# Local-attention half of a transformer block on one core: transposes into another bank, copies moved in the written orders, one bias sum on GpSimd

## The chip, the cores and the metric
The kernel runs on one core of a Trainium2 chip. The metric is the time of one execution on the device, in microseconds (us). TensorE (PE in the profile; PEld its weight loads), VectorE (DVE), ScalarE (ACT), GpSimd (POOL) and SyncE (SP, which only issues transfers) each work through a queue of their own, in order, and meet through semaphores.

## The reference
An input x (8 batches x 1024 tokens x 256) goes through two residual halves. Only the second is touched by the change:

```python
for l in range(2):                       # two layers, on the modulated, normalised x
    h = shift_token(x)                   # second half of the channels comes from the token before
    q, k, v = split(h @ wqkv[l])         # 8 heads of 64
    q, k = rotary_xpos(l2norm(q) * qs, l2norm(k) * ks)
    o = local_attention(q, k, v)         # windows of 128 tokens, each sees itself and the one before
    x = x + o @ wo[l]
    h = layernorm(shift_token(x))        # (h - mean) / sqrt(var + 1e-5) * g + b
    a, g = split(h @ w1[l] + b1[l])
    x = x + (a * gelu(g)) @ w2[l] + b2[l]
```

All of it is float32.

## The kernel before, in words
The first half (up to about 1951 us of the span) is another attention and is not changed. The second half treats the 8 batches as 4 pairs; one batch of a pair belongs to stream X, the other to stream Y, each with SBUF tiles and four PSUM banks of its own (X: 0 to 3, Y: 4 to 7; `bk` is the first). A unit `n` is one window of 128 tokens in one layer; layer `l = n % 2`, so each window goes through layer 0, then layer 1, and then the next window follows: 64 units in each stream.

The order of the work is written out by hand: each engine has a string of steps, and `rounds` goes through it once for every round. A step such as `uTX:0` is step `uT` of stream X for the unit of this round, `d0Y:1` is step `d0` of stream Y for the unit of the round before (the number is the lag). Every engine keeps to its own string; a step starts with waits on counting semaphores. The steps of a unit, in the order of the computation:
- `ln`, `le` (layer 0 only): mean and variance of x on VectorE (`ln`, L1282 and L1285), the power -0.5 on POOL (`ln`, L1531 and L1534), and the modulated `u0` on VectorE (`le`, L1289 to L1293).
- `uT` (TensorE, L792): two 128x128 transposes of the layer's input, `u0` or `u`, into bank bk + 2. `uTc` (VectorE, L1307 and L1310) copies them to SBUF, with the token shift.
- `ga`, `gb_`, `gb` (L799): queries and keys of heads 0-3 (a) and 4-7 (b) into banks bk and bk + 1. `v_`, `v` (L808): values into bank bk + 2. `sqa`, `sqb` (ScalarE, L1001) square, `ssa`, `ssb` (VectorE, L1315) sum, `rqa`, `rka`, `rqb`, `rkb` (POOL, L1541 and L1545) take the power; `rot`, `rs`, `ad`, `kn` with a or b (VectorE, L1323, L1329, L1335, L1341) are the rotation.
- `tqa`, `tka`, `tqb`, `tkb` (TensorE, L820) transpose, `qca`, `kca`, `qcb`, `kcb` (ScalarE, L1008 and L1012) copy to SBUF. `sa`, `sb` (TensorE, L830): the scores of four heads each; `sa` waits for `qca` and `kca`, `sb` for `qcb` and `kcb`.
- `m0`, `m1` (VectorE, L1353 and L1358): mask and maximum. `e0` to `e3` (ScalarE, L1019): exponentials of two heads each; `e0`, `e1` wait for `m0`, `e2`, `e3` for `m1`. `d0` to `d3` (VectorE, L1363 and L1366): reciprocal and scaling of two heads. `p0` to `p3` (TensorE, L838) transpose, `pc0` to `pc3` (ScalarE, L1025) copy.
- `o` (L847), `oc` (ScalarE, L1029), `wo_`, `wo` (L856): attention's output and its projection. `u1` (VectorE, L1370) adds the residual.
- `E`, `sh` (L863, L866): the token shift by matmul. `bnu`, `bns`, `ag` (VectorE, L1374, L1377, L1381): statistics; `rs` (POOL, L1549 and L1552): add 1e-5, power -0.5; `hl` (VectorE, L1385): normalise. `h` (TensorE, L871) transposes it, `hT` (ScalarE, L1033) copies.
- `w10` to `w12` (L881), `ge0` to `ge2` (ScalarE, L1041), `ac0` to `ac2` (VectorE, L1396), `w20` to `w22` (L891, into bank bk + 2): the feed-forward part.
- `ub` (VectorE, L1389): u = u1 + b2. `u2` (VectorE, L1402): u = u + the result of `w2`. `fin` (VectorE, L1300 and L1302), in layer 1, makes the output, which SyncE stores.

The semaphore `u2` counts two for every unit, one of `ub` and one of `u2`; `uT` of the next unit waits for both, in layer 0 too, since its bank is the one that `u2` reads. Around the change TensorE's order is `w21X:1 tkbY:1 w22X:1 uTX:0 sbY:1 gaX:0 p0Y:1 gb_X:0 p1Y:1 gbX:0 v_X:0 p2Y:1 vX:0 p3Y:1 tqaX:0 tkaX:0 oY:1`, and for the other stream `w22Y:1 wo_X:0 uTY:0 woX:0`.

Of the kernel before, what the change touches and what calls it, by code (L numbers as in the profile page):

```python
# [21 lines left out]
ALU = mybir.AluOpType  # L22
# [3 lines left out]
P = 128  # L26
B, T, D = 8, 1024, 256
# [39 lines left out]
def build(nc, x, Wa, ba, We, be, Wi, Wo, Wv, Wout, Wout_sw, head_vec, sgn, wqkv, q_scale, k_scale,  # L67
# [7 lines left out]
    with ctx:  # L75
# [7 lines left out]
        ident = res("ident", [P, P])  # L83
# [33 lines left out]
        b2_sb = res("b2_sb", [P, LAYERS, D])  # L117
# [36 lines left out]
        with ExitStack() as scope:  # L154
# [9 lines left out]
                u=tmp(f"u_s{s}", [P, D]),  # L164
# [408 lines left out]
        def _(pe):  # L573
# [207 lines left out]
            def step_pe(name, w, n):  # L781
# [3 lines left out]
                if name == "uT":  # L785
                    src = w["u0"] if l == 0 else w["u"]
                    if l == 0:
                        pe.wait_ge(w["s_ln0"], it * 3 + 3)
                    if n > 0:
                        pe.wait_ge(w["s_u2"], n * 2)  # L790
                    for k in range(DC):
                        mm = pe.transpose(psum[:, bk + 2, k * P:(k + 1) * P], src[:, k * P:(k + 1) * P], ident[:])  # L792
                    mm.then_inc(w["s_uT_ps"], 1)
                elif name in ("ga", "gb_", "gb"):
                    g = 0 if name == "ga" else 1
# [111 lines left out]
        def _(act):  # L907
# [87 lines left out]
            def step_act(name, w, n):  # L995
# [47 lines left out]
                else:  # L1043
# [10 lines left out]
        def _(dve):  # L1054
# [215 lines left out]
            def step_dve(name, w, n):  # L1270
# [32 lines left out]
                elif name == "uTc":  # L1303
# [4 lines left out]
                        .then_inc(w["s_uT"], 1)  # L1308
                    dve.wait_ge(w["s_uT"], n * 2 + 1)
                    dve.tensor_copy(uT[:, 0:2 * (P + 2)].rearrange("p (a n) -> p a n", a=2)[:, :, 0:P],  # L1310
                                    psum[:, bk + 2, 0:D].rearrange("p (a n) -> p a n", a=2)).then_inc(w["s_uT"], 1)
                elif name in ("ssa", "ssb"):
                    sq = w["pT"][:].rearrange("p h k n -> p (h k n)")[:, g * INNER:(g + 1) * INNER].rearrange("p (h d) -> p h d", d=LD)
                    dve.wait_ge(w[f"s_sq{g}"], n + 1)
# [22 lines left out]
                elif name in ("kna", "knb"):  # L1337
                    k = flat[:, g * 2 * INNER + INNER // 2:g * 2 * INNER + INNER].rearrange("p (h d) -> p h d", d=LD)
                    dve.wait_ge(w[f"s_rope{g}"], n * 4 + 3)
                    dve.wait_ge(w[f"s_rn{g}"], n * 4 + 2)  # L1340
                    dve.tensor_tensor(k, k, w["rn"][:, g * LH + LH // 2:(g + 1) * LH].unsqueeze(2).broadcast_to([P, LH // 2, LD]),  # L1341
                                      ALU.mult).then_inc(w[f"s_rope{g}"], 1)
                elif name in ("m0", "m1"):
                    g = int(name[1])
                    if n == 0:
                        dve.wait_ge(s_mask_in, 80)
                    dve.wait_ge(w[f"s_rn{g}"], n * 4 + 4)
                    dve.wait_ge(w[f"s_s_ps{g}"], n + 1)
                    dve.nop(nofuse=True)
                    for h in range(4 * g, 4 * g + 4):  # L1350
                        at, col, _ = score_place(h)
                        q = g * LH + h % 4
                        ins = dve.tensor_tensor_reduce(out=w["big"][:, h, :], in0=psum[:, bk + at, col:col + 2 * P],  # L1353
                                                       in1=maskv[:, 0 if t == 0 else 2 - own], scale=w["rn"][:, q:q + 1],
                                                       scalar=-3.4e38, op0=ALU.add, op1=ALU.max, accum_out=w["mx"][:, h:h + 1])
                    ins.then_inc(w[f"s_sm{g}"], 1)
                    dve.wait_ge(w[f"s_sm{g}"], n * 2 + 1)
                    dve.tensor_scalar(w["mx"][:, 4 * g:4 * g + 4], w["mx"][:, 4 * g:4 * g + 4], -1.0, None, ALU.mult) \  # L1358
                        .then_inc(w[f"s_sm{g}"], 1)
                elif name in ("d0", "d1", "d2", "d3"):  # L1360
                    m = int(name[1])
                    dve.wait_ge(w["s_exp"], n * 4 + m + 1)
                    dve.reciprocal(w["rz"][:, 2 * m:2 * m + 2], w["z"][:, 2 * m:2 * m + 2]).then_inc(w["s_pn"], 1)  # L1363
                    dve.wait_ge(w["s_pn"], n * 8 + 2 * m + 1)
                    for h in (2 * m, 2 * m + 1):
                        ins = dve.tensor_scalar(w["big"][:, h, :], w["big"][:, h, :], w["rz"][:, h:h + 1], None, ALU.mult)  # L1366
                    ins.then_inc(w["s_pn"], 1)
                elif name == "u1":
                    dve.wait_ge(w["s_wo_ps"], n + 1)
                    dve.tensor_tensor(w["u1"][:, l, own, :], psum[:, bk + 3, 0:D], (w["u0"] if l == 0 else w["u"])[:], ALU.add) \  # L1370
                        .then_inc(w["s_u1"], 1)
                elif name == "bnu":
                    dve.wait_ge(w["s_u1"], n + 1)
                    dve.bn_stats(w["st"][:, 0, :], w["u1"][:, l, own, 0:P]).then_inc(w["s_ln_ag"], 1)  # L1374
                elif name == "bns":
                    dve.wait_ge(w["s_sh_ps"], n + 1)
                    dve.bn_stats(w["st"][:, 1, :], psum[:, bk, 0:P]).then_inc(w["s_ln_ag"], 1)  # L1377
                elif name == "ag":
                    dve.wait_ge(w["s_ln_ag"], n * 3 + 2)
                    dve.nop(nofuse=True)  # L1380
                    dve.bn_aggr(w["mv"][:], w["st"][:].rearrange("p a n -> p (a n)")).then_inc(w["s_ln_ag"], 1)  # L1381
                elif name == "hl":
                    dve.wait_ge(w["s_ln_rs"], n * 2 + 2)
                    for k, src in ((0, w["u1"][:, l, own, 0:P]), (1, psum[:, bk, 0:P])):
                        dve.tensor_scalar(w["hl"][:, k * P:(k + 1) * P], src, w["mv"][:, 0:1], w["rs"][:], ALU.subtract, ALU.mult) \  # L1385
                            .then_inc(w["s_hl"], 1)
                elif name == "ub":
                    dve.wait_ge(w["s_u1"], n + 1)
                    dve.tensor_tensor(w["u"][:], w["u1"][:, l, own, :], b2_sb[:, l], ALU.add).then_inc(w["s_u2"], 1)  # L1389
                elif name in ("ac0", "ac1", "ac2"):  # L1390
                    j = int(name[2])
                    gl = w["pT"][:].rearrange("p h k n -> p (h k) n")
                    dve.wait_ge(w["s_gelu"], n * FC + 2 * j + 2)
                    for m, cc in enumerate((2 * j, 2 * j + 1)):
                        rows = FW if cc < FC - 1 else FR
                        dve.scalar_tensor_tensor(out=gl[0:rows, cc, :], in0=psum[0:rows, bk + G_BANK[j], (2 + m) * P:(3 + m) * P],  # L1396
                                                 scalar=b1_sb[0:rows, l, 0, cc:cc + 1], in1=gl[0:rows, cc, :],
                                                 op0=ALU.add, op1=ALU.mult).then_inc(w["s_act"], 1)
                elif name == "u2":
                    dve.wait_ge(w["s_w2_ps"], n + 1)  # L1400
                    dve.wait_ge(w["s_u2"], n * 2 + 1)
                    dve.tensor_tensor(w["u"][:], psum[:, bk + 2, 0:D], w["u"][:], ALU.add).then_inc(w["s_u2"], 1)  # L1402
                else:
                    raise ValueError(name)

            dve.wait_ge(s_wf, 16 * loads[1])
            dve.wait_ge(s_zero, 5)
            rounds(("rsbY:1 rotbY:1 adbY:1 ac0X:1 knbY:1 ac1X:1 ac2X:1 finY:2 m0Y:1 ubX:1 u2X:1 d0Y:1 uTcX:0 d1Y:1 m1Y:1 rsaX:0 "
                    "ssaX:0 d2Y:1 rotaX:0 d3Y:1 adaX:0 knaX:0 rotbX:0 ssbX:0 rsbX:0 adbX:0 m0X:0 u1Y:1 knbX:0 bnuY:1 bnsY:1 agY:1 "
                    "d0X:0 hlY:1 m1X:0 d1X:0 d2X:0 finX:1 d3X:0 lnY:0 ubY:1 ac0Y:1 ac1Y:1 leY:0 ac2Y:1 u2Y:1 uTcY:0 u1X:0 bnuX:0 "  # L1410
                    "lnX:-1 bnsX:0 agX:0 hlX:0 ssaY:0 rsaY:0 rotaY:0 adaY:0 knaY:0 leX:-1 ssbY:0"), step_dve)
# [3 lines left out]
        def _(gp):  # L1415
# [108 lines left out]
            def step_pool(name, w, n):  # L1524
# [90 lines left out]
```

## Time and profile before
| | us |
|---|---|
| median of 3 runs | 5147.08 (5144.16 to 5147.25) |
| the profiled execution | 5151.58, its span 5149.8 |
| PE busy, whole span | 4820.2 (94%) |
| DVE busy | 3885.7 (75%) |
| ACT busy | 2876.1 (56%) |
| POOL busy | 1178.6 (23%) |

Line 1 of the page gives the busy time of each engine; matmuls overlap, so a busy PE is not one at its peak. The second half of the kernel lies from about 1951 us on; a round in it takes about 49.3 us, and layer 0 and layer 1 alternate. A row in a timeline begins with its start in the span and its length; instructions on one engine may overlap at their ends. In brackets stands the idle time of that engine just before the row, and what ended it.

### The profile page before, as it was taken

The numbers are of one execution on the slowest core, as the hardware profiler recorded it, in microseconds if no ns is written. First come the engines' busy times: TensorE is split into PE (matmuls) and PEld (weight loads), VectorE is DVE, ScalarE is ACT, GpSimd is POOL, SyncE is SP. The second block draws the span as 40 slices with busy tenths as digits, with TensorE's granted clock in tenths as the row PEclk, the third lists the DMA queues.
The fourth block names the chain that finished last, engine by engine and source line by source line (L and its number), as shares of the span: only waits on it lengthen the run. The fifth ranks groups of instructions, "written<-read, shape, count | busy, mean of one in ns | idle before, by whom it ended". The sixth has DMA issues, their size and how long they took to land.

```text
span 5149.8 us, 85248 instructions
## 1 busy us (share of the span) xinstructions
PE 4820.2 (94%) x29996; PEld 2903.7 (56%) x29996; DVE 3885.7 (75%) x10911; ACT 2876.1 (56%) x6033; POOL 1178.6 (23%) x1722
## 2 busy tenths in 40 slices
PE   6799999999999997999999999999999999999998
PEld 2233333333333325777777777777777777777776
DVE  6688878788887865777777777777777777777776
ACT  1566666666666663555555555555555555555554
POOL 2202121121202002222222222222222222222222
PEclk7999999999999998999999999999999999999999
DMA  6333233233323311000000000000000000000000
GB/s 148 73 61 63 40 74 58 50 58 64 64 45 66 47 22 41 6 6 5 8 21 13 7 6 6 7 6 29 7 6 6 5 7 27 8 7 6 6 5 5
DMA packets 156588, 153.87 MB, mean 30 GB/s; under 512 B 25244, under 2 KB 148592, under 8 KB 156032
## 3 DMA queue, kind: packets, MB, share of 16 engines
q1 hardware_dynamic: 156160, 148.42, 14.1%
q8 instruction: 237, 3.88, 0.3%
q14 instruction: 191, 1.56, 0.1%
HBM read 103.49 MB, written 44.09 MB: 29 GB/s over the span
## 4 chain that ended last, share of the span: by engine, by line
PE 74%; DVE 12%; issue 4%; ACT 3%; DMA 2%; SPq 2%; POOL 2%; DVEq 0%; POOLq 0%; ACTq 0%
PE psum L881 13%; PE psum L645 8%; PE psum L663 7%; PE psum L799 7%; PE psum L675 6%; PE psum L891 5%; PE psum L847 5%; PE psum L808 4%; PE psum L838 4%; PE psum L830 3%; DVE big_s L1353 3%; DVE mx L1151 3%; PE psum L856 2%; PE psum L628 2%; PE psum L820 1%
## 5 line engine op out<-in xcount | busy, mean ns | idle before, releaser
L1151 DVE TENSOR_REDUCE mx<-psum 128x1 f32<-128x512 f32 x2048 | 1335.3, 687 | 302.0 <-PE psum L645 297.3
L955 ACT ACTIVATE pr<-psum 128x1024 f32<-128x1024 f32 x1024 | 1022.7, 1024 | 638.7 <-PE psum L663 627.5
L645 PE MATMUL psum<-stack 96*128 96x512 bf16 x2048 | 727.4, 389 | 63.3 <-DMA stack<-parts_d 21.5
L881 PE MATMUL psum<-hlT_s,w_sb 128*114 128x128 f32 (+1 forms) x6144 | 741.6, 274 | 30.0 <-ACT hlT_s L1033 30.0
L881 PEld LDWEIGHTS psum<-hlT_s,w_sb 128*114 128x114 f32 (+1 forms) x6144 | 702.9, 178 | 76.8 <-ACT hlT_s L1033 60.7
L1019 ACT ACTIVATE big_s<-big_s,mxl_s 128x256 f32<-128x256 f32 x1024 | 510.9, 502 | 301.5 <-DVE mxl_s L1358 301.5
L663 PE MATMUL psum<-stack 99*128 99x512 bf16 x2048 | 613.6, 381 | 22.7 <-DMA stack<-mrow 22.1
L645 PEld LDWEIGHTS psum<-stack 96*128 96x128 bf16 x2048 | 196.5, 96 | 749.8 <-DVE mx L1151 286.5
L1545 POOL TENSOR_TENSOR rn_s<-ss_s,neghalf 128x4 f32<-128x4 f32 x512 | 550.9, 1076 | 76.0
L675 PE MATMUL psum<-pr,vg 128*32 128x512 f32 x4096 | 546.7, 606 | 0.4 <-ACT pr L955 0.4
L799 PE MATMUL psum<-wqkv_sb,uT_s 128*128 128x512 f32 x1024 | 507.3, 608 | 0.7 <-DVE uT_s L1310 0.7
L1353 DVE CUSTOM_DVE_ANT_0 big_s<-psum,maskv,rn_s 128x256 f32<-128x256 f32 x1024 | 433.8, 482 | 66.6 <-PE psum L830 66.5
L1001 ACT ACTIVATE pT_s<-psum 128x512 f32<-128x512 f32 x256 | 152.4, 595 | 539.3 <-PE psum L799 539.3
L891 PE MATMUL psum<-w_sb,pT_s 114*128 114x256 f32 (+1 forms) x1536 | 408.1, 388 | 0.0
L1041 ACT ACTIVATE pT_s<-psum,b_sb 114x128 f32<-114x128 f32 (+1 forms) x768 | 238.8, 368 | 214.6 <-PE psum L881 213.9
L1541 POOL TENSOR_SCALAR ss_s<-ss_s 128x4 f32<-128x4 f32 x512 | 147.5, 288 | 922.2 <-DVE ss_s L1315 897.7
L1025 ACT ACTIVATE pT_s<-psum 128x512 f32<-128x512 f32 x512 | 294.4, 588 | 98.3 <-PE psum L838 98.3
L830 PE MATMUL psum<-kT_s,qT_s 64*128 64x256 f32 x2048 | 291.3, 403 | 61.4 <-ACT kT_s L1012 61.4
L838 PEld LDWEIGHTS psum<-ident,big_s 128*128 128x128 f32 x2048 | 250.1, 141 | 148.9 <-issue 102.3
L1366 DVE TENSOR_SCALAR big_s<-big_s,rz_s 128x256 f32<-128x256 f32 x1024 | 315.6, 351 | 18.5 <-DVE rz_s L1363 0.4
L1396 DVE SCALAR_TENSOR_TENSOR pT_s<-psum,b_sb,pT_s 114x128 f32<-114x128 f32 (+1 forms) x768 | 230.6, 346 | 113.9 <-ACT pT_s L1041 113.9
L838 PE MATMUL psum<-ident,big_s 128*128 128x128 f32 x2048 | 309.2, 274 | 6.9 <-DVE big_s L1366 6.8
(160 smaller groups left out, 6755.5 us busy)
## 6 DMA issues: line engine op xcount, KB each, us to landing
stack<-parts_d SPq DMA_DIRECT2D x384, 128.0 KB, 5.7
parts_d<-parts SPq DMA_DIRECT2D x64, 384.0 KB, 3.2
hn<-in_x SPq DMA_DIRECT2D x8, 1024.0 KB, 9.2
xr<-in_x SPq DMA_DIRECT2D x8, 1024.0 KB, 5.4
x_d<-xr SPq DMA_DIRECT2D x8, 1024.0 KB, 9.4
tab<-tab_d SPq DMA_DIRECT2D x32, 256.0 KB, 2.5
out_x<-o_s SPq DMA_DIRECT2D x64, 128.0 KB, 1.7
xs<-x_d SPq DMA_DIRECT2D x8, 896.0 KB, 7.5
```

The source lines that it names most:

```text
L645: pe.matmul(psum[:, to, :], stack[0:KS, g % 2, 0, u % 2, h, a * P:(a + 1) * P], stack[0:KS, g % 2, 1, kh, h, :], start=True, stop=True).th ...
L663: mm = pe.matmul(psum[:, h, :], stack[0:KS + PART, (u // 2) % 2, 1, kc // 4, h, (kc % 4) * P:(kc % 4 + 1) * P], stack[0:KS + PART, (u // 2 ...
L675: mm = pe.matmul(psum[h * VW:(h + 1) * VW, ACC, :], vg[:, (u // 2) % 2, kc, h, :], pr[:, e % 2, h, :], start=(kc == 0), stop=(kc == NT - 1))
L799: mm = pe.matmul(psum[:, bk + g, :], w["uT"][:, l, k * (P + 1):k * (P + 1) + P], wqkv_sb[:, l, k, 0:2 * INNER].rearrange("p (a g n) -> p g ...
L838: mm = pe.transpose(psum[:, bk + P_BANK[m], (2 * (h % 2) + kb) * P:(2 * (h % 2) + kb + 1) * P], w["big"][:, h, kb * P:(kb + 1) * P], ident[:])
L881: mm = pe.matmul(psum[0:rows, bk + G_BANK[j], m * P:(m + 1) * P], w1_sb[:, l, k, col:col + rows], w["hlT"][:, k, :], start=(k == 0), stop= ...
L891: mm = pe.matmul(psum[:, bk + 2, 0:D], hid[0:rows, cc, :], w2_sb[0:rows, l, cc, :], start=(cc == 0), stop=(cc == FC - 1))
L955: act.activation(pr[:, e % 2, 2 * pair:2 * pair + 2, :], psum[:, 2 * pair:2 * pair + 2, :], ACT.Exp, scale=DH ** -0.5).then_inc(s_exp, 1)
L1019: ins = act.activation(w["big"][:, h, :], w["big"][:, h, :], ACT.Exp, bias=w["mx"][:, h:h + 1], accum_out=w["z"][:, h:h + 1])
L1151: dve.tensor_reduce(mx[:, u % 2, m, kh:kh + 1], psum[:, src, :], AX.X, ALU.max).then_inc(s_max, 1)
L1353: ins = dve.tensor_tensor_reduce(out=w["big"][:, h, :], in0=psum[:, bk + at, col:col + 2 * P], in1=maskv[:, 0 if t == 0 else 2 - own], sca ...
L1545: gp.tensor_tensor(w["rn"][:, part], w["ss"][:, part], neghalf[:, 0:LH // 2], ALU.pow).then_inc(w[f"s_rn{g}"], 1)
```

## The change
Four edits, all in the second half.
1. `uT` of layer 0 writes bank bk + 3 in place of bk + 2, and `uTc` reads it there. It no longer waits for `u2` of the unit before, only for `ac0` of that unit (which had read bank bk + 3 last) and for `u0`. `v_`, the next to write bank bk + 2, waits for `u2` now. Layer 1 is as it was.
2. ScalarE: `qcbY` and `kcbY` stand ahead of `e0Y`. VectorE: `uTcX` stands ahead of `d0Y`.
3. `ubX` goes from VectorE to POOL, behind `rqbY`, with a further wait for the last `fin`. `ubY` stays on VectorE.
4. The addend 1e-5 of `rs` goes from POOL to VectorE, into `ag`, for both streams; POOL keeps the power.

```diff
                     if l == 0:
                         pe.wait_ge(w["s_ln0"], it * 3 + 3)
-                    if n > 0:
+                    if n > 0 and l == 0:
+                        pe.wait_ge(w["s_act"], (n - 1) * FC + 2)
+                    elif n > 0:
                         pe.wait_ge(w["s_u2"], n * 2)
                     for k in range(DC):
-                        mm = pe.transpose(psum[:, bk + 2, k * P:(k + 1) * P], src[:, k * P:(k + 1) * P], ident[:])
+                        mm = pe.transpose(psum[:, bk + 3 - l, k * P:(k + 1) * P], src[:, k * P:(k + 1) * P], ident[:])
...
                     if k == 0:
                         pe.wait_ge(w["s_uT"], n * 2 + 2)
+                        if n > 0:
+                            pe.wait_ge(w["s_u2"], n * 2)
...
-            rounds(("ge0X:1 ge1X:1 qcaY:1 kcaY:1 ge2X:1 e0Y:1 qcbY:1 kcbY:1 e1Y:1 sqaX:0 e2Y:1 e3Y:1 pc0Y:1 pc1Y:1 sqbX:0 pc2Y:1 "
+            rounds(("ge0X:1 ge1X:1 qcaY:1 kcaY:1 ge2X:1 qcbY:1 kcbY:1 e0Y:1 e1Y:1 sqaX:0 e2Y:1 e3Y:1 pc0Y:1 pc1Y:1 sqbX:0 pc2Y:1 "
...
-                                    psum[:, bk + 2, 0:D].rearrange("p (a n) -> p a n", a=2)).then_inc(w["s_uT"], 1)
+                                    psum[:, bk + 3 - l, 0:D].rearrange("p (a n) -> p a n", a=2)).then_inc(w["s_uT"], 1)
...
                 elif name == "ag":
-                    dve.wait_ge(w["s_ln_ag"], n * 3 + 2)
+                    dve.wait_ge(w["s_ln_ag"], n * 4 + 2)
                     dve.nop(nofuse=True)
                     dve.bn_aggr(w["mv"][:], w["st"][:].rearrange("p a n -> p (a n)")).then_inc(w["s_ln_ag"], 1)
+                    dve.wait_ge(w["s_ln_ag"], n * 4 + 3)
+                    dve.tensor_scalar(w["rs"][:], w["mv"][:, 1:2], LN_EPS, None, ALU.add).then_inc(w["s_ln_ag"], 1)
                 elif name == "hl":
-                    dve.wait_ge(w["s_ln_rs"], n * 2 + 2)
+                    dve.wait_ge(w["s_ln_rs"], n + 1)
...
-            rounds(("rsbY:1 rotbY:1 adbY:1 ac0X:1 knbY:1 ac1X:1 ac2X:1 finY:2 m0Y:1 ubX:1 u2X:1 d0Y:1 uTcX:0 d1Y:1 m1Y:1 rsaX:0 "
+            rounds(("rsbY:1 rotbY:1 adbY:1 ac0X:1 knbY:1 ac1X:1 ac2X:1 finY:2 m0Y:1 u2X:1 uTcX:0 d0Y:1 d1Y:1 m1Y:1 rsaX:0 "
...
                 elif name == "rs":
-                    gp.wait_ge(w["s_ln_ag"], n * 3 + 3)
-                    gp.nop(nofuse=True)
-                    gp.tensor_scalar(w["rs"][:], w["mv"][:, 1:2], LN_EPS, 1.0, ALU.add, ALU.mult).then_inc(w["s_ln_rs"], 1)
-                    gp.wait_ge(w["s_ln_rs"], n * 2 + 1)
+                    gp.wait_ge(w["s_ln_ag"], n * 4 + 4)
                     gp.nop(nofuse=True)
                     gp.tensor_tensor(w["rs"][:], w["rs"][:], neghalf[:, 0:1], ALU.pow).then_inc(w["s_ln_rs"], 1)
+                elif name == "ub":
+                    gp.wait_ge(w["s_u1"], n + 1)
+                    if l == 0 and it > 0:
+                        gp.wait_ge(w["s_oo"], it * 2)
+                    gp.nop(nofuse=True)
+                    gp.tensor_tensor(w["u"][:], w["u1"][:, l, t % 2, :], b2_sb[:, l], ALU.add).then_inc(w["s_u2"], 1)
...
-            rounds(("rqbY:1 rkaX:0 rqaX:0 rkbX:0 rqbX:0 rsY:1 lnY:0 lnX:-1 rsX:0 rkaY:0 rqaY:0 rkbY:0"), step_pool)
+            rounds(("rqbY:1 ubX:1 rkaX:0 rqaX:0 rkbX:0 rqbX:0 rsY:1 lnY:0 lnX:-1 rsX:0 rkaY:0 rqaY:0 rkbY:0"), step_pool)
```

## Rows read from the trace of the kernel before

**Rows 1.** Busy time of each engine in one pair of rounds (instructions in brackets).
```profile
3501.00:3599.59 98.59, 93.28 (x640) 70.18 (x639) 73.34 (x247) 53.90 (x148) 26.47 (x45) 1.00 0.04 12
```

**Rows 2.** Waits of TensorE, 2200 to 5100: us in total, times, longest.
```profile
PE psum L830 <- ACT kT_s L1012: 55.4, 89, 0.8
PE psum L871 <- DVE hl_s L1385: 36.2, 88, 0.8
PE psum L792 <- DVE u_s L1402: 33.8, 59, 0.7
```

**Rows 3.** Timeline of TensorE, rounds A and B: start, length, instructions, idle before.
```profile
3536.22 0.38 PE L820 MATMUL psum<-ident,big_s 128*128 128x128 f32 x2
...
3538.08 0.41 PE L792 MATMUL psum<-ident,u_s 128*128 128x128 f32 x2 [0.61 <-DVE u_s L1402]
...
3546.49 0.66 PE L820 MATMUL psum<-ident,big_s 128*128 128x128 f32 x4
...
3586.74 0.44 PE L792 MATMUL psum<-ident,u_s 128*128 128x128 f32 x2 [0.54 <-DVE u_s L1402]
3587.55 1.13 PE L830 MATMUL psum<-kT_s,qT_s 64*128 64x256 f32 x8 [0.37 <-ACT kT_s L1012]
```

**Rows 4.** Timeline of ScalarE, round A.
```profile
3536.33 0.51 ACT L1019 ACTIVATE big_s<-big_s,mxl_s 128x256 f32<-128x256 f32 x1 [1.20 <-DVE mxl_s L1358]
...
3537.60 0.37 ACT L1012 ACTIVATE kT_s<-psum 128x256 f32<-128x256 f32 x1
3537.86 0.50 ACT L1019 ACTIVATE big_s<-big_s,mxl_s 128x256 f32<-128x256 f32 x1
```

**Rows 5.** Timeline of VectorE, rounds A and B.
```profile
3536.13 0.17 DVE L1358 TENSOR_SCALAR mxl_s<-mxl_s 128x4 f32<-128x4 f32 x1
...
3537.50 0.42 DVE L1402 TENSOR_TENSOR u_s<-psum,u_s 128x256 f32<-128x256 f32 x1 [0.88 <-PE psum L891]
3537.84 0.16 DVE L1363 RECIPROCAL rz_s<-z_s 128x2 f32<-128x2 f32 x1
...
3539.09 0.16 DVE L1363 RECIPROCAL rz_s<-z_s 128x2 f32<-128x2 f32 x1
...
3539.81 0.48 DVE L1353 CUSTOM_DVE_ANT_0 big_s<-psum,maskv,rn_s 128x256 f32<-128x256 f32 x1
...
3542.20 0.76 DVE L1329 TENSOR_TENSOR big_s<-psum,tab 128x256 f32<-128x256 f32 x2 [0.48 <-ACT pT_s L1001]
...
3588.51 0.17 DVE L1363 RECIPROCAL rz_s<-z_s 128x2 f32<-128x2 f32 x1 [0.18 <-ACT big_s L1019]
...
3591.33 0.76 DVE L1329 TENSOR_TENSOR big_s<-psum,tab 128x256 f32<-128x256 f32 x2 [0.18 <-ACT pT_s L1001]
```

**Rows 6.** Timelines of POOL and VectorE, normalisation of stream Y.
```profile
3553.85 0.30 POOL L1549 TENSOR_SCALAR rs_s<-mv_s 128x1 f32<-128x1 f32 x1 [2.94 <-DVE mv_s L1381]
3554.30 0.55 POOL L1552 TENSOR_TENSOR rs_s<-rs_s,neghalf 128x1 f32<-128x1 f32 x1
...
3554.89 0.35 DVE L1385 TENSOR_SCALAR hl_s<-u_s,mv_s,rs_s 128x128 f32<-128x128 f32 x1 [0.52 <-POOL rs_s L1552]
```

**Rows 7.** Timelines of POOL and TensorE, normalisation of stream X.
```profile
3523.70 0.19 POOL L1549 TENSOR_SCALAR rs_s<-mv_s 128x1 f32<-128x1 f32 x1
3524.04 0.54 POOL L1552 TENSOR_TENSOR rs_s<-rs_s,neghalf 128x1 f32<-128x1 f32 x1
...
3525.34 0.44 PE L871 MATMUL psum<-ident,hl_s 128*128 128x128 f32 x2 [0.41 <-DVE hl_s L1385]
```

**Rows 8.** Timeline of POOL, round A, behind `rqbY`.
```profile
3543.71 0.39 POOL L1541 TENSOR_SCALAR ss_s<-ss_s 128x4 f32<-128x4 f32 x1 [9.89 <-DVE ss_s L1315]
```

**Rows 9.** Groups of instructions by line, POOL, 0 to 2050.
```profile
L1501 POOL TENSOR_TENSOR wga<-wfold,gA 128x512 f32<-128x512 f32 x8 | 10.2, 1270 | 52.6 <-DVE xr L1203 52.6
```

**Rows 10.** One line of VectorE: its durations in ns, least, median and most.
```profile
L1366 DVE TENSOR_SCALAR big_s<-big_s,rz_s x944: 345/352/357, 2204.5 to 5090.8; 128x256 f32<-128x256 f32 x189
```

## The prediction
> **What bounds the kernel now.** I call a round one pass of the written orders. A sum over two neighbouring rounds is needed, since the layer (and with it what is late) alternates. In [rows 1] one such pair takes 98.59 us; TensorE has matmuls in flight for 93.28 of them, VectorE works 73.34, ScalarE 53.90 and POOL 26.47, at a granted clock of 1.00. So TensorE bounds the second half, and time can only come from the 5.3 us in which it stands, or from what sits behind them. The view of waits says which these are [rows 2]: attention scores waiting for the copies of keys (55.4 us in 2900), the transposes of the normalised state waiting for VectorE's normalisation (36.2), and the transposes of the layer's input waiting for `u2` (33.8). The change aims at all three, but not at every instance of them; so I read one pair in order of time on each engine, and then moved its instructions. Round A (3501 to 3550) is the one in which stream X starts layer 0, round B (to 3599.6) the one in which it starts layer 1.
>
> **uTX into the other bank, layer 0 (round A).** TensorE ends w22X, idles 0.61 us for `u2`, then runs uTX, with sbY next [rows 3]. Afterwards uTX needs only u0, ready since the round before. So uTX moves up by the 0.61. sbY behind it needs kcbY: that copy ends at 3537.97 today [rows 4], and by itself would keep sbY at 3538.0, so that less than the 0.61 came through. The new wait of v_X for `u2` has the whole of TensorE's queue behind it, but `u2` is done at 3537.92 [rows 5] and v_X stands behind sbY, gaX, p0Y, gb_X, p1Y and gbX in the queue, sbY alone coming later than that: nothing. Stream Y's uTY already stands behind wo_X; the waits for `u2` number 59 [rows 2], one for each of X's rounds, so Y has none: nothing there. In round B uTX still waits for `u2` (0.54 idle, rows 3).
>
> **qcbY and kcbY ahead of e0Y.** Today the order is e0Y, qcbY, kcbY, e1Y [rows 4]. A copy holds ScalarE 0.26 (3537.60 to 3537.86), and 3536.33 to 3537.60 holds two exponentials and one copy, so e0Y is 1.01. New in A: tkbY's transposes end at 3536.60 [rows 3], qcbY starts at 3536.65, kcbY at 3536.91, and e0Y at 3537.17, 0.84 later than now, since its maxima were ready at 3536.30 [rows 5]. kcbY ends near 3537.3, so sbY is no longer late. In B the idle of 0.37 before sbY [rows 3] goes, and e0Y is hardly touched, as there the maxima come last.
>
> **uTcX ahead of d0Y, ubX off VectorE.** Removing ubX (0.34 of VectorE's time) gives nothing: u2X waits 0.88 for TensorE in A [rows 5]. What counts is when m1Y starts, because VectorE's rsaX, ssaX, d2Y, rotaX, d3Y, adaX, knaX follow m1Y in one run, and at its end tkaX needs knaX: TensorE's four transposes of tqaX and tkaX at 3546.49 take 0.66, tkbY's two 0.38 [rows 3], and I read a short wait for knaX in that.
> - A: today d0Y starts 3537.84, d1Y 3539.09, m1Y 3539.81 [rows 5]. d1Y holds VectorE 0.72, d0Y as much, and uTcX the other 0.53 of the 1.25 between d0Y and d1Y. New: uTcX 3537.84 (uTX is done by then), d0Y 3538.37, d1Y at 3539.09 again if e1Y allows it. e1Y starts 3537.17 + 1.01 = 3538.18 and ends, with its last read-out, at about 3539.28, so d1Y goes to 3539.33 and m1Y to 3540.05, 0.24 later. rsaX idles 0.48 today for the square of gaX; gaX is now 0.61 or more earlier, so rsaX starts where m1Y lets it: 0.48 - 0.24 = 0.24 earlier, up to 0.34 with the 0.10 by which a running queue starts the next instruction before the last one's end. I take 0.30.
> - B: uTX ends at 3586.74 + 0.44 = 3587.18. uTcX 3587.22, d0Y 3587.75, d1Y 3588.47, against 3588.51 today [rows 5]: VectorE's new wait for uTX costs what the old wait for e1Y cost; e1Y itself, no longer behind the copies (0.52), is done in time. rsaX's idle of 0.18 goes as its square comes 0.4 earlier. Gain 0.22 to 0.32, I take 0.26.
> So TensorE gets back 0.61 and 0.37 at the front, and most of that is lost again at p2Y, p3Y and tkaX: VectorE is late next.
>
> **The addend on VectorE.** For Y, POOL's add and its wait take 3553.85 to 3554.30, 0.45 [rows 6]. VectorE's narrow tensor_scalar is not in the trace at 128x1; the nearest row is 128x4 at 0.17 [rows 5], with 0.04 to start, 0.21. Saved 0.24, and hlY waits for exactly this power. But POOL's add took 0.30 there and 0.19 where VectorE stood still [rows 6, 7], because d0X's scalings run beside it; the power will now lie beside them. If it stretches by the same 0.11 the gain is 0.13; if it waits out one scaling (0.357, [rows 10]), it is -0.12 (0.24 - 0.36). Ends -0.12 and 0.24; I take 0.13, in both rounds, 0.26 together. After it hY and w10Y follow, both idle-marked today. d0X itself is put back 0.21, covered by the 0.52 that VectorE idles for the power [rows 6].
> For X, in the round with the extra statistics (lnX ahead of rsX on POOL), POOL's rsX add starts at 3523.70 straight behind lnX and the power at 3524.04 [rows 7]. VectorE's add is done long before, so the power starts at 3523.70: 0.34 of the 0.41 us that TensorE idles before hX. Ends 0.19 (the instruction alone) and 0.34; I take 0.34. In the other round hX shows no idle: nothing. The other hidden work moved by 0.34 still fits: in A VectorE has m0Y done at 3536.30, against u2X at 3537.16.
>
> **ubX on POOL.** Not in the trace at 128x256. A POOL tensor_tensor of 128x512 took 1.27 [rows 9]; at half its width it takes at most that, at least 0.42 (VectorE's own time for it); I use 0.7. POOL idles from 3533.82 (3543.71 - 9.89) to 3543.71 [rows 8], u2X needs `ub` by 3537.16: 2 us of cover at the worst. Its wait on the output's stores' semaphore was met a round before, and rkaX, behind it, needs ssaX much later. Cost 0. No DMA moves, SP's queue is not touched.
>
> **Sum.** 0.30 + 0.26 + 0.26 + 0.34 = 1.16 us for a pair, 32 pairs: 37 us. The profiled execution took 5151.6, the median of the runs 5147.1, so the sum is made on rounds of an execution 0.1% slower, which changes nothing in it: 5147.1 - 37 = **5110**. Its own ends: 0.34 + 0.32 + 0.48 + 0.34 = 1.48 (5100) and 0.24 + 0.22 - 0.24 + 0.19 = 0.41 (5134).
>
> **Rivals.**
> 1. TensorE keeps what it gets at the front: p2Y, p3Y and tkaX are not held by VectorE. 0.61 + 0.37 + 0.26 + 0.34 = 1.58, 51 us, 5096; more if the matmul queue hides less than I think. For it: no idle row stands in front of those transposes. Against: the stretched group at 3546.49. Chance 0.12.
> 2. The reordering is eaten by Y's softmax. e0Y's 0.84 passes in full to m1Y in A (0.48 - 0.84 = -0.36), and in B the 0.54 that VectorE stands for uTX passes too (0.18 - 0.54 = -0.36): -0.72 + 0.60 = -0.12, 4 us slower, 5151. For it: d1Y waits for e1Y in both rounds. Against: in A d0Y's place behind u2X leaves only e1Y's part to count. Chance 0.09.
> 3. Slower: POOL and VectorE shut each other out of SBUF. The power waits for all of d0X: d0X ends today at 3554.37 (3554.89 - 0.52, [rows 6]), so 3554.37 + 0.21 + 0.04 + 0.55 + 0.04 = 3555.21 for hlY, -0.32 per round. And `ub` holds VectorE for its 1.27: A has 1.22 in front of u2X (0.88 idle and ubX's 0.34), so -0.05; B has ubX's 0.34 for certain, so -0.93. 0.25 + (0.26 - 0.93) - 0.64 + 0.34 = -0.72 per pair, +23 us, 5170. With the power's part in full it decides from about 0.6 us of holding. Against: VectorE's scalings took 345 to 357 ns whether or not POOL worked beside them [rows 10]; for: POOL's own add was stretched. Chance 0.06. The Trainium skill, SBUF — State Buffer, section "Who interferes with whom", says that the shared port pair is an exclusive lock and the later one is blocked for the whole instruction, against a two-input or 2-port VectorE operation; by that rule the power in rows 6 would wait for a scaling to end, and this rival is its extreme. The 0.11 of stretch in the trace speaks for a block that is short, and on POOL's side.
> 4. POOL's power is stretched and the addend loses for Y (its lower end): 0.30 + 0.26 - 0.24 + 0.34 = 0.66, 5126. For it: the stretch in rows 6. Against: 0.36 is three times that stretch. Chance 0.15.
>
> **Numbers.** My forecast 0.58. Range for 8 in 10: 5093 to 5142, which takes in its ends, cases 1 and 4 and part of the way to case 2. Differences under 0.2% (10 us) are about what a measurement of this kernel can't tell from none. Faster by more: 0.58 + 0.15 + 0.12 = 0.85, same 0.09, slower 0.06.
>
> **What would show it.** Per pair 97.4 us; no idle before uTX in one of two rounds; the waits for keys falling from 1.87 to about 1.5 us a pair, with only those before sbX (0.75) left; rsX's power 0.34 earlier; new stalls before p2Y, p3Y or tkaX of 0.2 to 0.4. Wrong if m1Y starts more than 0.5 later behind w22X than now, if `ub` takes over 2 us, or if VectorE's instructions beside it stretch.

## The result, and the profile after

| | us |
|---|---|
| before, 4 runs | 5147.16 (5144.16 to 5147.73) |
| after, 4 runs | 5176.57 (5173.22 to 5179.21) |
| after divided by before | 1.0054, 95% interval 1.0042 to 1.0067 |
| profiled execution after | 5173.22, its span 5171.4 |

The change makes the kernel 29 us slower, where 37 us faster was forecast. The page's first line gives the busy time of each engine, its share of the span and the instructions:

```profile
PE 4847.7 (94%) x29996; PEld 2893.7 (56%) x29996; DVE 3889.9 (75%) x10975; ACT 2882.0 (56%) x6033; POOL 1195.4 (23%) x1658
```

POOL's busy time rose by 17 us, by what was given to it. PE's rose by 27 (4820.2 before), with the same 29996 matmuls; so matmul groups take longer, and the loss need not show as idle time. One pair of rounds, the view of [rows 1]:

```profile
3494.70:3594.20 99.50, 94.41 (x638) 70.01 (x638) 73.59 (x248) 54.10 (x149) 27.01 (x42) 1.00 0.10 30
```

The pair takes 99.50 in place of 98.59, 0.91 more, at the same granted clock of 1.00; times 32 it is 29 us, the measured loss. (The two profiled executions lie only 21.6 apart, 5171.4 and 5149.8, so for these two traces the pair is on the high side.) Within the pair TensorE's busy time rose by 1.13 and its idle time fell from 5.31 to 5.09. TensorE's waits in 2200 to 5100, the view of [rows 2] (total, times, longest):

```profile
PE psum L842 <- DVE big_s L1370: 48.3, 59, 1.1
PE psum L834 <- ACT kT_s L1016: 43.4, 58, 0.8
...
PE psum L794 <- DVE u_s L1408: 15.5, 30, 0.5
PE psum L875 <- DVE hl_s L1391: 12.5, 57, 0.6
```

All three waits at which the change aims fell: keys from 55.4 to 43.4, the normalised state from 36.2 to 12.5, `u2` from 33.8 to 15.5. In their place stands one that had no row before: the transposes `p2Y` wait for VectorE's scaling, 48.3 us, 59 times, once in each round. Waits alone therefore don't give the bill; it is made below from starts, which take in both the idle time and the stretched groups. Why `p2Y` waits is told by the timeline of ScalarE in round A. First the kernel before, between `ge2X` and `e0Y`; the second row here stands just ahead of the one that opens [rows 4]:

```profile
3533.21 0.63 ACT L1041 ACTIVATE pT_s<-psum,b_sb 114x128 f32<-114x128 f32 x2 [0.79 <-PE psum L881]
3533.85 1.28 ACT L1019 ACT_TABLE_LOAD   x1
```

Then the kernel after, same place of the round:

```profile
3543.29 0.38 ACT L1012 ACTIVATE qT_s<-psum 128x256 f32<-128x256 f32 x1 [2.81 <-PE psum L824]
3543.57 0.38 ACT L1016 ACTIVATE kT_s<-psum 128x256 f32<-128x256 f32 x1
3543.97 1.28 ACT L1023 ACT_TABLE_LOAD   x1
3545.26 0.51 ACT L1023 ACTIVATE big_s<-big_s,mxl_s 128x256 f32<-128x256 f32 x1
```

ScalarE must load another table between the Gelus (`ge`) and the exponentials. The load stands right ahead of the first exponential, whatever is in between. Before, that was in ScalarE's idle time behind `ge2X`, 1.2 us of it still left over [rows 4]. Now ScalarE idles 2.81 us for `tkbY` (both copies wait for both pairs of transposes), copies, and only then loads, 1.28 us, with `e0Y` behind it. VectorE in the same round:

```profile
3546.39 0.17 DVE L1367 RECIPROCAL rz_s<-z_s 128x2 f32<-128x2 f32 x1 [1.28 <-ACT big_s L1023]
...
3548.10 0.48 DVE L1357 CUSTOM_DVE_ANT_0 big_s<-psum,maskv,rn_s 128x256 f32<-128x256 f32 x1
```

And TensorE, first before, from w22X to oY in round A and in round B, then after, the same:

```profile
3536.44 1.03 PE L891 MATMUL psum<-w_sb,pT_s 114*128 114x256 f32 x4
...
3547.08 1.97 PE L847 MATMUL psum<-pT_s,v_s 128*64 128x128 f32 x32
...
3585.17 1.03 PE L891 MATMUL psum<-w_sb,pT_s 114*128 114x256 f32 x4
...
3596.21 1.97 PE L847 MATMUL psum<-pT_s,v_s 128*64 128x128 f32 x32
```

```profile
3543.09 1.03 PE L895 MATMUL psum<-w_sb,pT_s 114*128 114x256 f32 x4
3543.96 0.38 PE L794 MATMUL psum<-ident,u_s 128*128 128x128 f32 x2
3544.27 1.14 PE L834 MATMUL psum<-kT_s,qT_s 64*128 64x256 f32 x8
...
3552.05 0.66 PE L842 MATMUL psum<-ident,big_s 128*128 128x128 f32 x4 [1.11 <-DVE big_s L1370]
...
3553.97 0.90 PE L824 MATMUL psum<-ident,big_s 128*128 128x128 f32 x4
3554.79 1.97 PE L851 MATMUL psum<-pT_s,v_s 128*64 128x128 f32 x32
...
3592.67 1.03 PE L895 MATMUL psum<-w_sb,pT_s 114*128 114x256 f32 x4
...
3604.37 1.97 PE L851 MATMUL psum<-pT_s,v_s 128*64 128x128 f32 x32
```

`d0Y` waits 1.28 for `e0Y`, `m1Y` starts 5.01 behind w22X (3548.10 - 3543.09) where it was 3.37 (3539.81 - 3536.44), and `p2Y` makes TensorE stand 1.11. Behind it the group of `tqaX` and `tkaX` takes 0.90, where it took 0.66 [rows 3]. The front is as forecast: `uTX` and `sbY` follow w22X with no idle. In round B `uTX` still waits for `u2`, as forecast, `sbY` no longer waits, and `p2Y` makes TensorE stand 0.53.

The bill for a pair, from w22X's start to oY's: 11.70 in A (3554.79 - 3543.09) and in B (3604.37 - 3592.67), against 10.64 (3547.08 - 3536.44) and 11.04 (3596.21 - 3585.17) before: 1.06 + 0.66 = 1.72 lost. Behind that, `hY` idles 0.20 or 0.21 in place of 0.41 in both rounds, and `hX` none in place of 0.41: 0.83 won. 0.9 is left, the 0.91 of the pair.

### The profile page after: what moved, and what is told of

It reads as the page before. It is cut to its first block, busy times and chain, and to the rows that moved or that the text cites. A ratio compares the mean times of both kernels' runs of the same rounds, so it can differ in the third digit from the quotient of the medians.

```text
span 5171.4 us, 85310 instructions
## 1 busy us (share of the span) xinstructions
PE 4847.7 (94%) x29996; PEld 2893.7 (56%) x29996; DVE 3889.9 (75%) x10975; ACT 2882.0 (56%) x6033; POOL 1195.4 (23%) x1658
## 3 DMA queue, kind: packets, MB, share of 16 engines
q14 instruction: 191, 1.56, 0.1%
## 4 chain that ended last, share of the span: by engine, by line
PE 72%; DVE 13%; ACT 7%; issue 3%; DMA 2%; SPq 2%; POOL 0%; DVEq 0%; POOLq 0%; ACTq 0%
PE psum L885 13%; PE psum L645 8%; PE psum L663 7%; PE psum L675 7%; PE psum L895 6%; PE psum L851 5%; PE psum L801 4%; PE psum L834 4%; DVE big_s L1357 4%; PE psum L812 3%; PE psum L842 3%; DVE mx L1155 3%; ACT big_s L1023 3%; PE psum L824 2%; PE psum L860 2%
## 5 line engine op out<-in xcount | busy, mean ns | idle before, releaser
L663 PE MATMUL psum<-stack 99*128 99x512 bf16 x2048 | 614.0, 381 | 21.6 <-DMA stack<-mrow 21.0
L842 PEld LDWEIGHTS psum<-ident,big_s 128*128 128x128 f32 x2048 | 238.6, 142 | 234.7 <-DVE big_s L1370 194.3
```

The source lines that it names most:

```text
L663: mm = pe.matmul(psum[:, h, :], stack[0:KS + PART, (u // 2) % 2, 1, kc // 4, h, (kc % 4) * P:(kc % 4 + 1) * P], stack[0:KS + PART, (u // 2 ...
L842: mm = pe.transpose(psum[:, bk + P_BANK[m], (2 * (h % 2) + kb) * P:(2 * (h % 2) + kb + 1) * P], w["big"][:, h, kb * P:(kb + 1) * P], ident[:])
```

## The experiments

Ratios are against the kernel before on the same chip, with 95% intervals; its medians there were 5150.69 (e1 to e4), 5150.15 (e5 to e8) and 5151.78 us (e9 to e11). The theory: the table's load, put on the way to `e0Y`, costs all of it. The rival: it is the longer path of `e0Y` itself, or VectorE's new order, or POOL's sum, and the load changes nothing.

**e1_order_back**: the change, with ScalarE's old order.

```diff
-ge2X:1 qcbY:1 kcbY:1 e0Y:1 e1Y:1
+ge2X:1 e0Y:1 qcbY:1 kcbY:1 e1Y:1
```

> The changed kernel with ScalarE's order as it was before (e0Y ahead of qcbY and kcbY); all other edits stay. Theory T (the load of the exponential's table, 1.28 us, stands right ahead of the first exponential, so that the new order puts it behind kcbY and on the path to d0Y, m1Y and p2Y): all of the loss goes, and the other edits show. In round A sbY still waits for kcbY, 0.4 us gained; round B nothing; hY 0.2 in each round; hX 0.4: 1.2 us for a pair, 39 us under before, about 5108. Rival D (VectorE's uTcX ahead of d0Y, or the sum on POOL, makes VectorE late): little changes, about 5170.

Measured 5123.27 (5121.42 to 5126.0), ratio 0.9948 (0.9934 to 0.9961). The sign turns: ScalarE's order holds the loss. But 27 us are won, not what I expected. TensorE's row shows where the rest is:

```profile
3522.04 1.13 PE L834 MATMUL psum<-kT_s,qT_s 64*128 64x256 f32 x8 [0.74 <-ACT kT_s L1016]
```

`uTX` has moved up, but `sbY` behind it waits 0.74 for `kcbY`, which stands behind `e0Y`. From w22X to `sbY` is 1.99 (3522.04 - 3520.05), as before (3538.41 - 3536.44 = 1.97). `e0Y` itself starts 0.30 behind w22X here (at 3520.35), where it started 0.11 ahead of it [rows 4]: TensorE came forward by 0.41 at `hX`, and the maxima that `e0Y` waits for did not. The addend alone gives 31 us (e6 below); beside it the bank brings nothing more without the copies' move.

**e2_early_load**: the change, with one narrow exponential, whose result nothing reads, right behind `ge2X`. It pulls the load there.

```diff
+            warm = tmp("warm", [P, 1])
...
+                elif name == "warm":
+                    act.activation(warm[:], zero[:, 0:1], ACT.Exp)
...
-ge2X:1 qcbY:1 kcbY:1 e0Y:1 e1Y:1
+ge2X:1 warmY:1 qcbY:1 kcbY:1 e0Y:1 e1Y:1
```

> The changed kernel with one narrow exponential (128x1, its result unused) right behind ge2X, ahead of qcbY and kcbY, whose only use is to draw the table's load forward to there. T: the load lies in ScalarE's idle time again, and the prediction's own sum comes out with the measured terms of the addend: 0.30 + 0.26 + 0.42 + 0.41 = 1.4 us for a pair, 45 us under before, about 5102. D: no change, about 5176.

Measured 5100.66 (5097.72 to 5104.27), ratio 0.9903 (0.989 to 0.9917): 50 us faster than before, 1.5% faster than the change. ScalarE, TensorE and VectorE in round A:

```profile
3508.26 0.62 ACT L1048 ACTIVATE pT_s<-psum,b_sb 114x128 f32<-114x128 f32 x2 [0.79 <-PE psum L886]
3508.90 1.28 ACT L1009 ACT_TABLE_LOAD   x1
3510.19 0.20 ACT L1009 ACTIVATE warm<-zero 128x1 f32<-128x1 f32 x1
3511.69 0.38 ACT L1015 ACTIVATE qT_s<-psum 128x256 f32<-128x256 f32 x1 [1.29 <-PE psum L825]
3511.97 0.38 ACT L1019 ACTIVATE kT_s<-psum 128x256 f32<-128x256 f32 x1
3512.23 0.51 ACT L1026 ACTIVATE big_s<-big_s,mxl_s 128x256 f32<-128x256 f32 x1
```

```profile
3511.49 1.03 PE L896 MATMUL psum<-w_sb,pT_s 114*128 114x256 f32 x4
3512.36 0.38 PE L795 MATMUL psum<-ident,u_s 128*128 128x128 f32 x2
3512.67 1.13 PE L835 MATMUL psum<-kT_s,qT_s 64*128 64x256 f32 x8
...
3521.75 1.42 PE L852 MATMUL psum<-pT_s,v_s 128*64 128x128 f32 x22
```

```profile
3515.06 0.48 DVE L1360 CUSTOM_DVE_ANT_0 big_s<-psum,maskv,rn_s 128x256 f32<-128x256 f32 x1
```

The load fits into the idle time with 1.29 to spare. `e0Y` starts 0.74 behind w22X, `m1Y` 3.57, oY 10.26.

**e3_order_alone**: the kernel before, with ScalarE's new order and nothing else.

```diff
-ge2X:1 e0Y:1 qcbY:1 kcbY:1 e1Y:1
+ge2X:1 qcbY:1 kcbY:1 e0Y:1 e1Y:1
```

> The kernel before with ScalarE's new order alone (qcbY and kcbY ahead of e0Y). T: e0Y starts 2.1 us later in A (0.84 for the copies, 1.28 for the load), and uTcX stands behind d0Y here, so gaX is late by 1.6 in A and 1.1 in B: 2.7 us for a pair, 87 us over before, about 5234. D: this order does no harm, 5130 to 5150.

Measured 5267.53 (5265.61 to 5271.26), ratio 1.0228 (1.0214 to 1.0242): 117 us slower. The late `e0Y` costs even more here, as `uTcX` stands behind `d0Y`, and so `gaX` is late with it. It is some 30 us more than expected; the last section says where most of them are.

**e4_bank_alone**: the kernel before, with the bank and its waits alone.

```diff
-                    if n > 0:
+                    if n > 0 and l == 0:
+                        pe.wait_ge(w["s_act"], (n - 1) * FC + 2)
+                    elif n > 0:
                         pe.wait_ge(w["s_u2"], n * 2)
...
-                        mm = pe.transpose(psum[:, bk + 2, k * P:(k + 1) * P], src[:, k * P:(k + 1) * P], ident[:])
+                        mm = pe.transpose(psum[:, bk + 3 - l, k * P:(k + 1) * P], src[:, k * P:(k + 1) * P], ident[:])
```

> The kernel before with layer 0's transposes in bank bk + 3 alone, with its waits. Both theories: uTX and sbY move up in A, but gaX waits for uTcX, which stands behind d0Y on VectorE and ends at 3539.18: gaX 0.24 earlier, 8 us under before, about 5139. If TensorE's gain came through in full (0.61): 5127; if it doesn't count at all: 5147.

Ratio 0.9985 (0.9976 to 0.9994), 7 us faster: clearly there and small. The wait for `u2` in A turns into one for keys; before there were 89 of these, 55.4 us [rows 2], and now

```profile
PE psum L834 <- ACT kT_s L1016: 64.6, 118, 0.7
```

**e5_order_alone_early_load**: e3 with e2's narrow exponential.

```diff
-ge2X:1 e0Y:1 qcbY:1 kcbY:1 e1Y:1
+ge2X:1 warmY:1 qcbY:1 kcbY:1 e0Y:1 e1Y:1
```

> The kernel before with ScalarE's new order alone, and the narrow exponential (128x1, its result unused) right behind ge2X that draws the table's load forward. It differs from the run with the new order alone (5267.5, against 5150.7 before) by that one instruction. T: only the 0.84 us of the two copies is left; by hand A loses nothing (rsaX's idle of 0.48 takes up m1Y's 0.48), B gains 0.2 to 0.3: 6 us under before, about 5144. A rival that puts the harm on the copies' delay of e0Y: at least half of the 117 us stays, over 5205.

Ratio 1.0002 (0.9993 to 1.001). Against e3, 117 us slower, the early load takes away all of the loss, so the copies' own delay of `e0Y` is not what costs. Nor does ScalarE's order bring anything where it stands alone, though I expected 6 us: `sbY` no longer waits, but then `gaX` does, for a copy that stands behind `d0Y`. Waits of TensorE:

```profile
PE psum L831 <- ACT kT_s L1015: 44.1, 59, 0.7
...
PE psum L800 <- DVE uT_s L1313: 5.5, 29, 0.2
```

**e6_addend_alone**: the kernel before, with the addend 1e-5 in VectorE's `ag`, and POOL's `rs` without its own add.

```diff
+                    dve.wait_ge(w["s_ln_ag"], n * 4 + 3)
+                    dve.tensor_scalar(w["rs"][:], w["mv"][:, 1:2], LN_EPS, None, ALU.add).then_inc(w["s_ln_ag"], 1)
...
-                    gp.tensor_scalar(w["rs"][:], w["mv"][:, 1:2], LN_EPS, 1.0, ALU.add, ALU.mult).then_inc(w["s_ln_rs"], 1)
-                    gp.wait_ge(w["s_ln_rs"], n * 2 + 1)
```

> The kernel before with the addend on VectorE alone. hY's idle was 0.21 shorter in both rounds of the changed kernel, hX's 0.41 gone in one: 0.8 us for a pair, 26 us under before. If sbY in A, whose kcbY hangs on m0Y and so on VectorE's own chain, takes part of hX's gain back: 13 to 26 under.

Measured 5119.53 (5118.31 to 5125.25), ratio 0.9942 (0.9928 to 0.9955): 31 us faster, 0.96 per pair. TensorE's waits for the normalised state fall from 36.2 [rows 2] to

```profile
PE psum L871 <- DVE hl_s L1387: 12.6, 60, 0.3
```

**e7_early_load_d0_first**: e2, with `uTcX` behind `d0Y` again.

```diff
-m0Y:1 u2X:1 uTcX:0 d0Y:1 d1Y:1
+m0Y:1 u2X:1 d0Y:1 uTcX:0 d1Y:1
```

> The version with the early load (5100.7), with VectorE's order of d0Y ahead of uTcX as it was before. Prediction's own step (uTcX ahead of d0Y lets gaX start on time, m1Y hardly moves): gaX waits 1.0 us more in A, 0.2 more in B, partly taken up by what VectorE is late anyway: 0.4 to 0.9 us a pair worse, 5114 to 5130. If VectorE's order counts for nothing: 5101. If d0Y first is better, since p2Y waits for it: under 5095.

Measured 5124.74, ratio 0.9951 (0.9938 to 0.9963), 24 us slower than e2. TensorE waits where e2 does not, in A and in B:

```profile
3525.89 1.98 PE L802 MATMUL psum<-wqkv_sb,uT_s 128*128 128x512 f32 x4 [0.94 <-DVE uT_s L1317]
...
3574.62 1.98 PE L802 MATMUL psum<-wqkv_sb,uT_s 128*128 128x512 f32 x4 [0.20 <-DVE uT_s L1317]
```

**e8_early_load_ub_back**: e2, with `ubX` on VectorE again.

```diff
-m0Y:1 u2X:1 uTcX:0
+m0Y:1 ubX:1 u2X:1 uTcX:0
...
-rqbY:1 ubX:1 rkaX:0
+rqbY:1 rkaX:0
```

> The version with the early load (5100.7), with ubX back on VectorE ahead of u2X. ubX holds VectorE 0.34 in front of u2X, where it idles 0.80 in A and 0.42 in B for TensorE: no difference, 5098 to 5104. If POOL's sum was a cost (shared access to SBUF), this is faster, under 5095; if it was a gain, slower, over 5107.

Measured 5099.69 (5098.57 to 5100.91), ratio 0.9901 (0.9888 to 0.9915), the same as e2. Where `ubX` runs is worth nothing here.

**e9_copy_in_its_place**: e2, with a copy as the narrow instruction: same place, same cost, but it needs no new table.

```diff
-                    act.activation(warm[:], zero[:, 0:1], ACT.Exp)
+                    act.activation(warm[:], zero[:, 0:1], ACT.Copy)
```

> The version with the early load (5100.7), but its narrow extra instruction is a copy in place of an exponential: the same order, the same extra 128x1 instruction, no table drawn forward. T: the load is back behind kcbY, the full loss is back, 5170 to 5180. If the extra instruction itself helped (its place in the queue, a wait that it shifts): near 5101.

Measured 5180.49 (5177.31 to 5182.46), ratio 1.0055 (1.0043 to 1.0068), the change's own 1.0054. ScalarE's load is back behind `kcbY`:

```profile
3549.19 0.20 ACT L1009 ACTIVATE warm<-zero 128x1 f32<-128x1 f32 x1
...
3552.39 0.38 ACT L1019 ACTIVATE kT_s<-psum 128x256 f32<-128x256 f32 x1
3552.78 1.28 ACT L1026 ACT_TABLE_LOAD   x1
```

So it is where the table is loaded, and not one instruction more in ScalarE's queue. (1.0055 - 0.9903) x 5151 = 78 us, or 2.4 us for a pair: two loads of 1.28, almost in full.

**e10_values_split**: e2, with oY cut in two around `tqaX` and `tkaX`, and `vcX` ahead of `qcaX`. It was to win back what TensorE waits for `knaX` there.

```diff
-p3Y:1 tqaX:0 tkaX:0 oY:1 saX:0
+p3Y:1 oaY:1 tqaX:0 tkaX:0 obY:1 saX:0
...
-pc3Y:1 qcaX:0 vcX:0 kcaX:0 ocY:1
+pc3Y:1 vcX:0 qcaX:0 kcaX:0 ocY:1
```

> The version with the early load (5100.7), with oY on TensorE split in two halves and tqaX, tkaX between them; ScalarE copies the values vcX ahead of qcaX. If VectorE's chain, up to knaX, is what is late next (the prediction's claim; the four transposes take 0.90 and 0.78 there against 0.60 unhindered), TensorE works through the first half of oY in that time and takes tkaX on time: up to 0.5 us in A and 0.35 in B, 5074 to 5090. If TensorE's own queue bounds this stretch: 5098 to 5104. If kcaX now comes too late for saX: over 5104.

A miss: 5098.58 (5096.8 to 5106.15), ratio 0.9902 (0.9887 to 0.9917), no different from e2. TensorE and VectorE in round A:

```profile
3514.74 1.09 PE L852 MATMUL psum<-pT_s,v_s 128*64 128x128 f32 x16
3515.76 0.66 PE L825 MATMUL psum<-ident,big_s 128*128 128x128 f32 x4
3516.35 0.88 PE L852 MATMUL psum<-pT_s,v_s 128*64 128x128 f32 x12
```

```profile
3514.73 0.43 DVE L1349 TENSOR_TENSOR big_s<-big_s,rn_s 128x256 f32<-128x256 f32 x1
```

`knaX` is done at 3515.16, ahead of the transposes, and they still take 0.59 from start to start (0.66 with the tail). So this is their own length, and only the longer group of e2 holds a wait. That wait is gone here and nothing is won: oY's two halves take 2.04 from start to start, where e2's oY took 1.90. From `p3Y` to `saX`, A is 0.10 shorter than in e2 (3.19 against 3.29) and B 0.12 longer (3.16 against 3.04).

**e11_copy_order_alone**: the kernel before, with `uTcX` ahead of `d0Y`.

```diff
-m0Y:1 ubX:1 u2X:1 d0Y:1 uTcX:0 d1Y:1
+m0Y:1 ubX:1 u2X:1 uTcX:0 d0Y:1 d1Y:1
```

> The kernel before with VectorE's order alone (uTcX ahead of d0Y). By hand: in A uTX ends at 3538.46, so uTcX, d0Y, d1Y end 0.67 later and m1Y starts 0.67 later, of which rsaX's idle takes 0.48 to 0.58: 0.1 to 0.2 worse; B nothing. 3 to 6 us over before, 5150 to 5156. The same order gave 24 us beside the early load and the new order on ScalarE (5124.7 to 5100.7), so the two orders would be worth something only together.

Ratio 1.0008 (0.9999 to 1.0017): nothing, or 3 us slower.

What the parts add up to. Alone against before: bank -7, addend -31, ScalarE's order with the early load +1, VectorE's order +3. Their sum is -34; together, with the early load (e2), -50. The two orders are worth something only in company: without VectorE's, 24 us of e2 are lost (e7); without ScalarE's, 23 (e1 against e2, in which the load is early by itself). Each frees TensorE from a wait that the other would put back. In both of those runs layer 0's bank was the new one as well, and alone each order ran with the old one, so no run shows how much of the 23 and 24 needs the bank too.

## Why the prediction was wrong, step by step

- **The step that failed** is "qcbY starts at 3536.65, kcbY at 3536.91, and e0Y at 3537.17, 0.84 later than now". It moved two copies past an exponential and counted only rows with an output of their own. The load at 3533.85 belongs to the exponential (its line is `e0`'s) and moves with it, from idle time into the path. `e0Y` was put at 0.73 behind w22X (3537.17 - 3536.44). Measured in the change: 2.17 (3545.26 - 3543.09), 1.44 more. Of that the load is 1.28; most of the rest is `kcbY`, which took 0.40 to the load's start (3543.97 - 3543.57) where 0.26 was counted. Measured with the load behind `ge2X` (e2): 0.74.
- **What follows from `e0Y`.** m1Y was to start 3.61 behind w22X (3540.05 - 3536.44): 3.57 in e2 (3515.06 - 3511.49), 5.01 in the change. The prediction named m1Y more than 0.5 later as what would prove it wrong; it is 1.64 later than before. The path itself, from `e1Y` over `d1Y` and m1Y to VectorE's run, was read right, and along it the late `e0Y` reached `p2Y`.
- **uTX and the order, 0.30 (A) and 0.26 (B).** In e2, w22X to oY takes 10.26 and 10.69 (3570.33 - 3559.64), against 10.64 and 11.04: 0.38 and 0.35. The mechanism held once the load was out of the way, and each size was 0.08 or 0.09 too low.
- **"most of that is lost again at p2Y, p3Y and tkaX".** At the front e2 gains 0.79 in A (w22X to `sbY` 1.97 before, 1.18 in e2) and 0.47 in B (2.38, 3587.55 - 3585.17, and 1.91); 0.38 and 0.35 reach oY. So 0.41 and 0.12 are lost again between, in e2 in the group of `tqaX` and `tkaX`: from `p3Y`'s start to oY's is 1.39 in A (3521.75 - 3520.36), against 1.03 before (3547.08 - 3546.05). But the sign by which I knew it, "a short wait for knaX" in the 0.66 of [rows 3], was misread: that is the group's own length (e10), and before there was no wait in it. The conclusion held in A; for B it is small.
- **The addend, 0.26 for Y and 0.34 for X.** Measured 0.42 (0.41 to 0.20 or 0.21 in each of two rounds) and 0.41: 0.83 in place of 0.60. Alone (e6) 31 us, 0.96 per pair. Both parts were too small, X's by 0.07. For Y the rows are these, one of before and two of after:

```profile
3553.48 0.21 DVE L1381 BATCH_NORM_AGGREGATE mv_s<-st_s 128x2 f32<-128x12 f32 x1
```

```profile
3561.19 0.21 DVE L1385 BATCH_NORM_AGGREGATE mv_s<-st_s 128x2 f32<-128x12 f32 x1
...
3561.73 0.63 POOL L1555 TENSOR_TENSOR rs_s<-rs_s,neghalf 128x1 f32<-128x1 f32 x1 [3.12 <-DVE rs_s L1387]
```

From `ag` to the power is 0.54 (3561.73 - 3561.19) in place of 0.82 (3554.30 - 3553.48), 0.28 saved where I had 0.24; and the power takes 0.63 in place of 0.55, 0.08 of stretch where I had 0.11.
- **ubX on POOL, 0.** It takes 725 ns (0.7 was assumed), and with the load early it is worth nothing in either place (e8).
- **The sum.** With the load where it was, 0.38 + 0.35 + 0.83 = 1.56 per pair, 50 us; measured -50 (e2). That is also the 51 us of rival 1, by coincidence: the front does lose again, and the addend is larger. The change: 0.9 lost, 29 us.

Rival 3 forecast the right side and almost the right time (5170), by a mechanism that isn't there. VectorE's scalings and POOL's sum, durations in ns, least, median and most, in the kernel after:

```profile
L1370 DVE TENSOR_SCALAR big_s<-big_s,rz_s x1024: 340/351/371, 1969.5 to 5145.9; 128x256 f32<-128x256 f32 x171
...
L1561 POOL TENSOR_TENSOR u_s<-u_s,b_sb x64: 718/725/731, 1996.2 to 5133.1; 128x256 f32<-128x256 f32 x64
```

The scalings stand at a median of 351, 352 before [rows 10], with POOL's sum and power beside them. Y's power, beside them each time, is stretched by the 0.08 above, and never by a whole scaling: the longest of all the powers took 682 ns, 555 before. Whether it is held for a moment or runs slower, these rows don't tell. Rival 2, the softmax eating the front's gain, is what happened in form (0.7 lost from w22X to oY per pair was its price, 1.72 the true one), but its cause was a late `e0Y` by 0.84, and e2 has just that lateness and wins. Rival 1 falls with the 0.41 lost in A, rival 4 with the addend's 31 us.

The Trainium skill, "ScalarE: Activation LUTs", section "Step-by-step: what each stage is for", says that the compiler places a load right before the activation that needs a set which isn't active; "Table sets: the hidden batching unit" adds that cheap functions, copy among them, are in every set. Both agree with the rows: the load stands right ahead of the first exponential in before, after and e2, and the copies run on either side of it. I had not weighed these two sentences together; they say that a copy moved ahead of an exponential moves ahead of its load too. On the same page the Trainium skill, in the section "What ACT_TABLE_LOAD costs", gives 1283 ns for the load, which the trace has too (1.28), and some 1380 ns of drain in addition. That does not show here: `kcbY` ends at 3543.95, the load runs from 3543.97 to 3545.25, `e0Y` starts at 3545.26, and a load costs 1.2 us of the kernel's time (78 us for 64 of them), not 2.66.

## What to carry to other kernels

Before a step is moved on ScalarE, look for every table load in its timeline and see whose line it bears: it goes with the first instruction that needs the new table, and is free only while idle time stands directly ahead of that one. Where it isn't, a one-column activation of the new kind, placed at the end of the old kind's work, puts the load there for 0.20 us; here that turned 29 us slower into 50 us faster (e2, the fastest here with e8 and e10). And price moves on several engines together: the two orders gave about nothing each alone and 23 or 24 us each beside the other and the new bank.

## What the hardware showed that I had not expected

In e3, TensorE idles 1.44 to 1.64 us before `gaX` in 63 rounds, for the copy behind `d0Y`, and in 15 of them the four matmuls behind it took 3.37 to 3.63 us, where the others took 1.98. The timeline of two rounds, and the busy times in the two stretches (the last three columns: granted clock, DMA share, GB/s):

```profile
3547.59 3.61 PE L799 MATMUL psum<-wqkv_sb,uT_s 128*128 128x512 f32 x4 [1.63 <-DVE uT_s L1310]
...
3497.03 1.98 PE L799 MATMUL psum<-wqkv_sb,uT_s 128*128 128x512 f32 x4 [1.58 <-DVE uT_s L1310]
```

```profile
3547.50:3551.00 3.50, 3.40 (x4) 1.40 (x5) 2.51 (x13) 0.00 (x0) 0.00 (x0) 0.51 1.05 377
3497.00:3498.85 1.85, 1.82 (x4) 0.82 (x5) 1.81 (x10) 0.00 (x0) 0.00 (x0) 1.00 0.03 9
```

The granted clock was 0.51 in the one, the lower of the two levels (1.2 of 2.4 GHz), and 1.00 in the other, behind nearly the same idle. 15 times 1.5 is 23 of the 30 us by which e3 was slower than expected. In e7 the same group stood behind 0.20 to 0.94 of idle in 63 rounds, and in before, after and e2 behind none; there it never took more than 1.99. The transfers of the first stretch are not the cause: in 12 of the 15 the DMA share was 0.02 or less. Of the 15, 11 stood behind the longer idle of 1.63 and 4 behind one of 1.57 or 1.58. What sets one round apart from the next with the same idle stays open. So a wait on TensorE can cost twice: itself, and a slower clock behind it.
